# Ten of the low parts of the item table made by GpSimd instead of VectorE in the first pooling pass

## The reference

```
mask      = (sequence_ids != 0)[..., None]
pooled    = where(mask, table[clip(sequence_ids - 1, 0)], 0).sum(1) / max(mask.sum(1), 1)
user_rep  = pooled @ W_rec.T + b_rec
retrieved = table[retrieved_indices].mean(axis=1)
gate      = sigmoid(concat([user_rep, retrieved]) @ gate_W.T + gate_b)
fused     = gate * user_rep + (1 - gate) * retrieved
logits    = fused @ proj_W.T + proj_b
```

## Time and profile before

| | us |
|---|---|
| three runs: lowest, median, highest | 2227.30, 2282.04, 2289.00 |
| the profiled execution | 2237.35 |
| its span, from first to last instruction | 2235.6 |
| PE busy | 2126.1 (95%) |
| DVE busy | 1556.0 (70%) |
| POOL busy | 1116.2 (50%) |
| ACT busy | 765.1 (34%) |

### The profile page before, as it was taken

How to read it: one execution, slowest core, us unless ns; L and a number is a source line. 1 busy time by engine, 2 the same in 40 slices (tenths; PEclk the granted TensorE clock), 3 DMA queues, 4 the chain that set the end, 5 groups by cost and what they waited for, 6 DMA issues and landing times.

```text
span 2235.6 us, 31374 instructions
## 1 busy us (share of the span) xinstructions
PE 2126.1 (95%) x12548; PEld 1090.5 (49%) x12548; DVE 1556.0 (70%) x1751; ACT 765.1 (34%) x972; POOL 1116.2 (50%) x830
## 2 busy tenths in 40 slices
PE   5678999999999999997999999999999999999999
PEld 4554555555555554443444444444444444444444
DVE  8998899778877875363467876558678872655554
ACT  5866776444445442132311212121211221221211
POOL 5683555488568856777256665436466700000000
PEclk9759999999999999998999999999999999999999
DMA  8998999799779989897389988749799973676765
GB/s 303 334 207 259 309 317 316 216 252 256 226 234 243 255 236 374 261 355 245 121 299 316 311 298 286 247 150 331 228 325 335 379 237 122 226 239 217 240 217 180
DMA packets 221999, 586.77 MB, mean 262 GB/s; under 512 B 21792, under 2 KB 120992, under 8 KB 218528
## 3 DMA queue, kind: packets, MB, share of 16 engines
q0 software_dynamic: 77632, 218.16, 35.4%
q1 hardware_dynamic: 91424, 264.21, 34.6%
q10 hardware_dynamic: 52800, 102.41, 12.1%
HBM read 448.21 MB, written 136.48 MB: 262 GB/s over the span
## 4 chain that ended last, share of the span: by engine, by line
PE 88%; DVE 6%; ACT 3%; issue 1%; DVEq 1%; DMA 1%; another core or an unknown queue 0%; SPq 0%; ACTq 0%
PE pooled_ps L1033 35%; PE pooled_ps L959 28%; PE count_ps L1033 9%; PE count_ps L941 7%; PE count_ps L987 5%; PE count_ps L977 2%; ACT counts L783 2%; DVE row_hots L566 2%; DVE keys L568 1%; DMA mid<-emb 1%; ACT counts L777 1%; DVE ring L573 0%; PE count_ps L982 0%; DVE keys L553 0%
## 5 line engine op out<-in xcount | busy, mean ns | idle before, releaser
L959 PE MATMUL pooled_ps<-mid,ring 128*128 128x512 f16 x3136 | 736.0, 382 | 29.3 <-issue 10.0
L447 POOL DMA_INDIRECT gathered<-emb,ret_rows x466 | 576.5, 1237 | 301.6 <-DVE gathered L608 145.6
L959 PEld LDWEIGHTS pooled_ps<-mid,ring 128*128 128x128 f16 x3136 | 293.9, 98 | 347.9 <-issue 53.2
L753 DVE SCALAR_TENSOR_TENSOR ring<-pooled_ps,out_scale,counts 128x500 f32<-128x500 f32 x320 | 234.6, 737 | 275.1 <-PE pooled_ps L1033 257.1
L1033 PE MATMUL pooled_ps<-counts,keys 128*128 128x500 f16 x1920 | 417.2, 375 | 0.9 <-DVE mid L591 0.9
L469 POOL DMA_INDIRECT gathered<-emb,ret_rows x184 | 342.6, 1862 | 148.6 <-DVE keys L568 84.5
L1033 PE MATMUL pooled_ps<-counts,mid 128*128 128x500 f16 x1920 | 412.8, 374 | 2.2 <-DVE counts L648 2.2
L566 DVE TENSOR_TENSOR row_hots<-pair_columns,keys 128x2048 f16<-128x2048 f16 x256 | 313.0, 1223 | 105.7 <-PE count_ps L941 88.9
L941 PE MATMUL count_ps<-keys,row_hots 128*128 128x98 f16 x4096 | 282.9, 226 | 50.1 <-DVE keys L568 34.1
L941 PEld LDWEIGHTS count_ps<-keys,row_hots 128*128 128x128 f16 x4096 | 254.0, 108 | 128.0 <-DVE keys L568 44.8
L859 ACT ACTIVATE counts<-counts,strip_scale 128x2000 f16<-128x2000 f32 x75 | 147.0, 1960 | 492.7 <-PE pooled_ps L1033 272.5
(11 more groups left out here) (99 smaller groups left out, 1056.7 us busy)
## 6 DMA issues: line engine op xcount, KB each, us to landing
logits<-ring ACTq DMA_DIRECT2D x100, 1000.0 KB
ring<-emb_parts SPq DMA_DIRECT2D x147, 512.0 KB
counts<-proj_t SPq DMA_DIRECT2D x75, 1000.0 KB
counts<-emb SPq DMA_DIRECT2D x14, 1792.0 KB, 12.0
mid<-emb SPq DMA_DIRECT2D x49, 512.0 KB
emb_parts<-ring SPq DMA_DIRECT2D x49, 512.0 KB
counts<-proj_b SPq DMA_DIRECT2D x75, 250.0 KB
gathered<-emb,ret_rows POOLq DMA_INDIRECT x666
```

What stands on the lines that cost most here:

```text
L447: pool.indirect_dma_start(slots[group][:, a], None, source, column(block, r * SLOT + a))\
L753: dve.scalar_tensor_tensor(rows[:, r % ROW_SLOTS, v], logit_ps[n % BANKS][:, 0:W], out_scale[:, t % 2, j // GROUP_BLOCKS:j // GROUP_BLOCKS ...
L959: last = pe.matmul(pooled_ps[:, m], ring_v[:, p % RING, c, part, m * P:(m + 1) * P], cvt[:, p % CVT, c], start=(i == 0 and c == 0 and part ...
```

## The change

Ten pairs, 6, 9, 12 and so on to 33 (`POOL_LOWS`), get their low part from GpSimd. It multiplies the stage slot by the scale in place (f32), drains, and subtracts the high part into the ring: two instructions of 128x1024 elements. DVE leaves these ten out. The gathers of turns 7 to 11 no longer wait for hots; one block's four gathers stand behind each of the ten. Turn 12 stands behind them. Whoever waited for a low part (SP's store, the PE, GpSimd's own wait before it reuses `mid`) now waits for the semaphore of the engine that makes it. SP's order of stores and loads is the same. All ten pairs are multiples of 3 and so lie in stage slot 0.

```diff
+POOL_LOWS = tuple(range(6, 34, 3))
+        def wait_low(eng, i):
+            if i in POOL_LOWS:
+                eng.wait_ge(pool_low_made, POOL_LOWS.index(i) + 1)
+            else:
+                eng.wait_ge(low_made, i + 1 - sum(1 for n in POOL_LOWS if n < i))
...
             def store_parts(i):
-                sp.wait_ge(low_made, i + 1)
+                wait_low(sp, i)
...
                     if kind == "low":
-                        pool.wait_ge(low_made, NP)
+                        wait_low(pool, NP - 1)
+                        wait_low(pool, POOL_LOWS[-1])
...
-            for turn in range(turns):
+            for turn in range(7):
                 if turn > 0:
                     pool.wait_ge(hots_made, 9 * turn)
                 for block in range(LANES):
                     gather_lane(block, turn)
+            for j, i in enumerate(POOL_LOWS):
+                pool.wait_ge(high_made, i + 1)
+                pool.tensor_scalar(stage[:, i % STAGE], stage[:, i % STAGE], small[:, 1:2], None, ALU.mult)
+                pool.drain()
+                pool.tensor_tensor(ring_v[:, i % RING, :, 1, :], stage[:, i % STAGE], ring_v[:, i % RING, :, 0, :],
+                                   ALU.subtract).then_inc(pool_low_made, 1)
+                gather_lane(j % LANES, 7 + j // LANES)
+            for turn in range(7 + len(POOL_LOWS) // LANES, turns):
+                for block in range(LANES):
+                    gather_lane(block, turn)
...
-                    if g == 0 and i + 3 < NP:
+                    if g == 0 and i + 3 < NP and i + 3 not in POOL_LOWS:
                         split_low(i + 3)
...
                     if g == 0:
-                        pe.wait_ge(low_made, i + 1)
+                        wait_low(pe, i)
```

More of the change, by code:

```diff
@@ L249, in pooling_program @@
         low_made = sem("low_made")
+        pool_low_made = sem("pool_low_made")
         ring_stored = [sem(f"ring_stored{s}") for s in range(RING)]
```

## The result

The changed kernel takes 2335.94 us (median of four runs, 2329.88 to 2349.32), the kernel before, beside it on the same chip, 2257.0 (four runs, 2227.3 to 2289.0). The ratio is 1.048, 95% interval 1.042 to 1.054: slower, and outside the predicted range of 2225 to 2310. On three other chips, further down, it was 1.027 to 1.029 (on one of them in a single run). On some chips single executions come out longer at a lower granted clock; the ratios leave these out, the medians do not. The profiled execution is the one of 2331.56 us, span 2329.8.

What follows compares the result with a forecast made beforehand. In pass 0 PE, DVE and transfers lay close together, the PE busiest. 0 (DVE) + 12 (slot 0's late loads) + 0 (turn 12 hidden) = +12 us on 2260 gave 2272 us, range 2225 to 2310.

Steps and rivals of the forecast that it cites:

- Bound and reserves of pass 0: Pass 0: PE, DVE and transfers lie close together, so at most 3.4 us could be won.
- DVE's relief is worth nothing: Pass 0: ten low parts, 12.8 us, leave DVE, which already waits for the PE; gain taken as 0.
- The two operations, 4.4 us: GpSimd's multiplication and subtraction for each low part: 4.4 us together, bounded by 1.9 and 8.2.
- two semaphores and a drain 0.6: Between slot 0's high part and its next load: semaphores and GpSimd's drain together take 0.6 us.
- GpSimd fits, barely; from 5.1 us on it sets the pace: Pass 0: GpSimd needs 13.1 of 13.83 us per three pairs; its two operations may take 5.1 us together.
- GpSimd becomes the bound: Rival: GpSimd's operations take long, up to 8.2 us, and set pass 0's pace; 2320 us, chance 0.08.
- no idle before L501, PE waiting for POOL: Sign in the profile that GpSimd sets the pace: no wait before its multiplication, and the PE waits for it.
- The slot's loop, +12: Stage slot 0: later loads make its loop 15.65 us against 13.83; 18 us, less 3 and 3, gives +12.
- ACT waiting 20 us or more for loads: Sign for the forecast: ACT's idle time for DMA rises from 9.6 us to 20 or more.
- the pace of 4.7 to 4.9 us a pair: Sign for the forecast: pass 0 runs at 4.7 to 4.9 us a pair up to pair 36, 4.6 after.
- Mutual exclusion, 15 in 100, +30: Rival: in pass 0 DVE and GpSimd stop each other on SBUF; +30 us, 2290 us, chance 0.15.
- Turn 12 and the first lane are hidden: End of pass 0: turn 12's gathers done by 328.5 us, before DVE's lane at 332.95; cost 0.

Runs made afterwards that it cites:

- b2_before: The unchanged kernel, run once for a profile beside the changed kernel on another chip; 2211.72 us.
- e2_sem: Changed kernel with the drain between GpSimd's two operations replaced by a semaphore; 2227.53 us, ratio 1.0073 to the kernel before.
- e13_sem: Repeat on another chip of the changed kernel with a semaphore instead of the drain; 2228.01 us, ratio 1.0067 to the kernel before.
- e8_four: Changed kernel with four low parts on GpSimd instead of ten, drain and gather places kept; 2232.88 us, ratio 1.0104 to the kernel before.
- e11_excl: Kernel before, plus ten pairs of GpSimd operations on scratch tiles behind turns 7 to 11, semaphores for drains; 2279.84 us, ratio 1.0132.
- e4_scratch: Changed kernel with DVE making all low parts and GpSimd's operations and drain on unused scratch tiles; 2293.96 us against 2244.17 before.
- a4_after: The changed kernel itself, repeated on another chip; 2274.06 us, ratio 1.0289 to the kernel before.
- a2_after: The changed kernel itself, run once more for a second profile; 2274.74 us against 2210.53 before.
- e12_probe: Kernel before, plus probes at the end of GpSimd's queue: gathers with landing waits, drains and the two operations; 2211.59 us against 2211.43.
- e9_probe: Kernel before, plus probes at the end of GpSimd's queue: gathers alone, with drain, with operation and drain; 2214.56 us against 2210.53.
- e3_gathers_after: Changed kernel with the gathers of turns 7 to 11 moved behind all ten GpSimd low parts; 2312.77 us, ratio 1.025 to the kernel before.

## Why the prediction was wrong

The forecast was +12 us on a kernel of 2260; measured were +79 on the first chip (2257.0 before) and +62.6 on the quietest. Up to some 30 of the 79 us, those of pass 3, are not shown to be the change's; the 60.5 us of pass 0 by themselves lie beyond the forecast, and beyond the 2310 too (2257.0 + 60.5 = 2317.5). Its steps:

1. **Bound and reserves of pass 0**: held. Three engines close together, at most 3.4 us to win; no version won any.
2. **DVE's relief is worth nothing**: held, and more. In the semaphore version DVE has nine low parts less in nine rounds, 11.5 us, and its other instructions are 19.5 us longer (39 x 0.285 + 39 x 0.195 + 18 x 0.042 against b2_before, 183 to 316 us): the change loads DVE rather than relieves it.
3. **The two operations, 4.4 us**: 4.98 alone, 6.1 beside a busy DVE (3.57 + 2.58). That is inside the bounds of 1.9 to 8.2, but beyond the 5.1 us from which, by the prediction itself, GpSimd sets the pace. That the sum came near was in part luck: the first was put at 1.9 us and took 2.85, the second at 2.5 and took 2.13.
4. **"two semaphores and a drain 0.6"**: this is the step that failed. The drain by itself had no row and no bounds; I gave it a share of a round sum, though every other new thing was bounded from both sides. It took 4.1 to 6.0 us in nine rounds, because four gathers stood unlanded ahead of it, and 4.75 in the first, where none did. With its 5.2 us the round is 3.5 + 5.2 + 2.6 + 8.7 = 20 us by the prediction's own sum (19.14 measured, as the first operation overlaps the last gather's record), not 13.1.
5. **GpSimd fits, barely; from 5.1 us on it sets the pace**: the threshold was right. The two operations with what stands between them took 11.3. So the rival "GpSimd becomes the bound" came true, given 8 in 100, by the pause and not by long operations; "no idle before L501, PE waiting for POOL" is what the groups and waits show. By its own rule, ten for each microsecond beyond 5.1, it would have given +62: measured +60.5 in pass 0. Without the drain, at 6.1 us, GpSimd is still just beyond its spare time: its rounds are 14.78 us in e2_sem and 15.18 in e13_sem.
6. **The slot's loop, +12**: its mechanism shows in e8_four (45.1 us of waits for loads) and, with 22.7 us of them, in e2_sem. In the changed kernel it is covered by the larger bound: slot 0's loads were issued 13.8 us behind the high part instead of 6.15, and the next high part in the slot began 5.4 us after them, in nine of ten cases behind a wait of ACT for the load. The 9.5 us of the prediction were right for the kernel before (9.7 in the mean of the ten, 7.8 to 14.0), but did not carry over. In e2_sem, with the DMA engines at a share of 1.01 from 205 to 350 us, the two are 8.4 and 6.3 us, a loop of 14.7 where the prediction had 15.65: two errors of 2 to 3 us that nearly cancel. Why a load that is issued late takes less time is not shown. The sign that it named, ACT waiting 20 us or more for loads, came true (22.3 us), and yet something else set the pace; the pace of 4.7 to 4.9 us a pair did not (19.14 / 3 = 6.4). What I had overlooked is that SP's queue holds the loads of slots 1 and 2 behind the late one.
7. **Mutual exclusion, 15 in 100, +30**: real. A DVE instruction that meets an operation of GpSimd takes 2.65 to 3.18 us for 1.21 to 1.28. That is the rule that the prediction named (the Trainium skill, SBUF — State Buffer, "Who interferes with whom"), and this case's runs agree with it. Without anyone waiting for GpSimd's results it cost 19 us in e11_excl and 9 to 10 in e4_scratch.
8. **Turn 12 and the first lane are hidden**: no longer. The last low part started 49 us later than forecast (355.55 against 307), the gathers of turn 12 ended at 386, and DVE waited 5.84 us in the finished lane. The sum had named this cover and its price rightly, but not its loss. Even without the drain DVE waited there, 4.4 us in e2_sem and 4.1 in e13_sem.

Of the 62.6 us the drain is 46.0, shown by exchanging it alone. The remaining 16.6 are near the 12 forecast, but that does not bear the forecast out. What acts there is a GpSimd round of 15.18 for 13.83 us (9 x 1.35 = 12.2 in e13_sem, 8.6 in e2_sem), DVE's instructions stretched by GpSimd's, late loads, and the wait at the finished lane. These push on the same pace and were not separated; their single prices (9 to 19 for operations that nobody waits for, 22 for four low parts with drain) do not add up to it and need not.

The PE's clock differs too: from 205 to 350 us it was granted 0.87 of full speed in a4_after and 0.99 in e13_sem. It is not shown that this costs anything: in these rounds GpSimd waits for nobody, and the PE waits for it. How much of the 46 us it is, if any, wasn't tried.

None of the versions beats the kernel before. The semaphore one is the best of the changed, and still 0.7% slower.

## What to carry to other kernels

On an engine that issues its own gathers, order two of its instructions by a semaphore and not by a drain; the drain costs the landing of the gathers that were issued before it. (The semaphore orders the two instructions alone; that was all that was needed here.) Bound every added instruction that has no row, the ones that compute nothing first, and test the sum against the engine's spare time with each at its upper end: here 0.7 us of spare time stood beside a price that nobody had measured. Work given to GpSimd is not taken off DVE where DVE's instructions are stretched by it; compare what leaves DVE (1.28 us) with what comes back (1.4 to 1.9 us per meeting, up to two meetings a low part; in e2_sem 19.5 us came back for the 11.5 that left).

## What the runs showed of the hardware that I had not expected

- GpSimd's drain waits for the landing of its gathers: of 26 rounds with four gathers ahead in a2_after, a4_after and e12_probe, the next instruction began 0.30 us after the last landing in 25. The pauses were 3.1 to 5.6 us behind one gather (e9_probe), 2.9 behind four and a multiplication, 4.1 to 6.7 in pass 0; 0.15 with no gather ahead, 0.5 to 1.2 behind landed ones. This does not explain the first drain of the changed kernel, of e3_gathers_after and of e8_four, 4.75 us each time, when the last gather had ended over 28 us earlier. What that one waits for stays open.
- On GpSimd the operation with one tile as input was the slower one: 2.85 us (2.77 with a constant) for 1024 f32 elements a partition, against 2.13 for the subtraction of an f16 from an f32 tile. Setting the same tile took 0.97. Beside a busy DVE the multiplication took 3.57 in the mean and the subtraction 2.58.
- A DVE instruction can take 2.5 times as long (1.28 to 3.18 us) when it meets a GpSimd operation on SBUF, and keeps its time beside the 1.86 us that GpSimd spends on issuing a gather.
- The PE's waits came with a lower clock: with the PE busy 130 of 165 us it was granted 0.88 (1.00 before, busy 162.6), and the eight matmuls behind a wait of 4.38 us took 3.57 us at 0.50, against 1.89 for a like group at 205.81, at 1.00.
